# Row maxima as a 97th row of the contraction in a fused decoder layer pair

## What is computed

```python
x = _layernorm(x + _L0_attn_ref(x, ...), axis=-1)       # splat attention, 256 keys, head width 16
x = _layernorm(x + _L0_xattn_ref(x, ctx_512, ...), axis=-1)   # cross attention, 120 keys, width 16
x = _layernorm(x + _L0_ffn_ref(x, ...), axis=-1)
x = _layernorm(x + _L1_attn_ref(x, ...), axis=-1)       # causal attention, 256 keys, width 16
x = _layernorm(x + _L1_xattn_ref(x, ctx_512, ...), axis=-1)   # self (256 keys) and cross (120), width 32
x = _layernorm(x + _L1_ffn_ref(x, ...), axis=-1)
```

```python
attn = jnp.einsum('bqhd,bkhd->bhqk', Q, K) * SCALE
attn = jax.nn.softmax(attn, axis=-1)
O = jnp.einsum('bhqk,bkhd->bqhd', attn, V)
```

## Time and profile before

| what | value |
|---|---|
| median of 3 runs | 3753.8 us (3750.38 to 3755.05) |
| the profiled execution's own time | 3753.18 us |
| its span, first to last instruction | 3751.0 us |
| mean granted clock of TensorE, share of 2.4 GHz | 0.924 |
| instructions | 89546 |

### The profile page before, as it was taken

One profiled execution on the slowest core, in us unless ns is written; L12 is line 12 of the kernel. 1 busy time (PEld: TensorE's weight loads), 2 busy tenths in 40 slices (PEclk: granted clock), 3 DMA queues, 4 the chain that ended last, 5 costly groups with the idle time before them and its releaser, 6 DMA issues. The chain is left out here.

```text
span 3751.0 us, 89546 instructions
## 1 busy us (share of the span) xinstructions
PE 3123.4 (83%) x34864; PEld 2456.7 (65%) x34864; DVE 2699.4 (72%) x6135; ACT 2105.0 (56%) x4254; POOL 978.4 (26%) x1793
## 2 busy tenths in 40 slices
PE   1989888888888978888988888798988897988886
PEld 1767666766676757766766666676756676766664
DVE  6868676777676767767777667687777677768765
ACT  4745665555556554564565555646655556466542
POOL 1312341122223321231133222212343113124310
PEclk9999899999899989989998988999999999999987
DMA  6211211112112121121121111212121112122110
GB/s 199 70 55 56 79 61 53 45 45 67 55 54 72 48 62 41 50 67 55 48 72 56 54 53 38 70 45 71 60 67 60 39 41 68 48 62 71 60 37 6
DMA packets 362006, 221.49 MB, mean 59 GB/s; under 512 B 102497, under 2 KB 333298, under 8 KB 361586
## 3 DMA queue, kind: packets, MB, share of 16 engines
q1 hardware_dynamic: 361586, 215.76, 19.0%
HBM read 122.23 MB, written 93.32 MB: 57 GB/s over the span
## 5 line engine op out<-in xcount | busy, mean ns | idle before, releaser
L1158 ACT ACTIVATE p<-bank,p_log 128x512 f32<-128x512 f32 (+2 forms) x1280 | 748.3, 585 | 1122.3 <-PE bank L850 1019.3
L1712 POOL TENSOR_TENSOR prob<-p,prob 120x256 f16<-120x256 f32 (+2 forms) x512 | 451.7, 882 | 1650.9 <-ACT prob L1159 1650.5
L1159 ACT ACTIVATE prob<-bank,p_log 128x512 f16<-128x512 f32 (+2 forms) x1280 | 749.3, 585 | 0.0
L1417 DVE TENSOR_REDUCE negm<-bank 128x2 f16<-128x512 f32 (+1 forms) x1280 | 674.8, 568 | 98.9 <-PE bank L813 89.2
L1347 DVE TENSOR_TENSOR prob<-p,prob 128x512 f16<-128x512 f32 (+2 forms) x768 | 485.6, 641 | 92.6 <-ACT prob L1159 88.5
L720 PE MATMUL bank<-w_exp,ident_h 128*128 128x512 f16 x1280 | 418.9, 411 | 101.7 <-DMA k_ring<-k_heads 85.8
L829 PE MATMUL bank<-q_ring,k_ring 80*128 80x256 f16 (+4 forms) x2048 | 445.1, 284 | 40.8 <-ACT raw L1105 14.4
L850 PE MATMUL bank<-ident_h,negm 128*128 128x256 f16 (+2 forms) x2560 | 440.7, 259 | 0.0
L1721 POOL TENSOR_SCALAR_AFFINE_SELECT probm<-prob 128x128 f16<-128x128 f16 x1024 | 326.7, 357 | 308.9 <-DVE prob L1347 308.9
L813 PE MATMUL bank<-k_ring,q_ring 80*128 80x256 f16 (+4 forms) x2560 | 368.5, 259 | 34.8 <-DVE negm L1417 34.2
L813 PEld LDWEIGHTS bank<-k_ring,q_ring 80*128 80x128 f16 (+1 forms) x2560 | 236.5, 104 | 234.2 <-issue 51.5
(11 more groups left out here) (299 smaller groups left out, 6190.1 us busy)
## 6 DMA issues: line engine op xcount, KB each, us to landing
q_ring<-q_heads SPq DMA_DIRECT2D x768, 40.0 KB, 2.2
q_heads<-q_made SPq DMA_DIRECT2D x96, 256.0 KB, 2.4
k_heads<-k_made SPq DMA_DIRECT2D x96, 256.0 KB, 2.3
q_ring<-q_heads SPq DMA_DIRECT2D x512, 48.0 KB, 2.2
k_ring<-k_heads SPq DMA_DIRECT2D x512, 40.0 KB, 2.2
q_heads<-q_made SPq DMA_DIRECT2D x144, 128.0 KB, 1.8
k_heads<-k_made SPq DMA_DIRECT2D x144, 128.0 KB, 1.8
k_ring<-k_heads SPq DMA_DIRECT2D x256, 48.0 KB, 2.2
```

What stands on the lines that cost most here:

```text
L1158: act(p32[0:n, g % PBUF32, 0:cols], ps[0:n, 0:cols], ACT.Exp, bias=p_log[0:n, :], scale=a.scale)
L1159: act(prob[0:n, 0, g % PBUF, 0:cols], ps[0:n, 0:cols], ACT.Exp, bias=p_log[0:n, :], scale=a.scale).then_inc(a_done, one(a_done))
L1417: v.tensor_reduce(negm[:, h * NT:(h + 1) * NT], ring_v[bank_of(e, v_full)][:, :].rearrange("p (t n) -> p t n", t=NT)[:, :, 0:ATTNS[k].keys ...
L1712: g.tensor_tensor(prob[0:n, 1, m % PBUF, 0:cols], p32[0:n, m % PBUF32, 0:cols], prob[0:n, 0, m % PBUF, 0:cols], ALU.subtract).then_inc(pp_ ...
```

## The change

The maximum becomes a row of the contraction. `q_ring` and `k_ring` get a 97th row: ones in `k_ring`, set once, and the negated maxima in `q_ring`. So the exact scores need no product of their own for the maxima. To bring the maxima from columns (a query per partition) to a row (a query per column), TensorE makes four products per pair with the identity, each of 128 columns, into a bank of `ring_a` (`maxima_to_row`), and ScalarE copies one partition of that bank, 512 elements, to row 96 of `q_ring` (`row_of_maxima`). Both are the last piece of the step in which the maxima are taken. The wait for the maxima moves from `exact_scores` to `maxima_to_row`, and `exact_scores` waits for ScalarE's copy.

For this the 16-wide heads are stacked to 96 rows as well, with a third plane of zeros, so the fills carry 96 rows and twelve stores of zeros at the start stand in the place of eight. For causal heads the mask product now closes the group. The core of the diff:

```diff
-        self.stacked = 96 if dim == 32 else 80
+STACKED = 96
...
-        q_ring, k_ring = (sb(f"{what}_ring", [96, SLOTS, PAIR, TOK], F16) for what in "qk")
+        q_ring, k_ring = (sb(f"{what}_ring", [STACKED + 1, SLOTS, PAIR, TOK], F16) for what in "qk")
...
-                        for plane in (3, 4):
+                        for plane in (3, 4, 5):
...
+                step(g.memset(k_ring[STACKED:STACKED + 1, :, :, :], 1.0))
...
+                def maxima_to_row(pair):
+
+                    ps = slot("a", "row", pair[0] // PAIR)
+                    e.wait_ge(*moved("max", pair[1]))
+                    for at, g in enumerate(pair):
+                        for i in range(NT):
+                            column = ORDER[g][2] * NT + i
+                            c = (at * NT + i) * P
+                            last = mm(ps[:, c:c + P], negm[:, column:column + 1].broadcast_to([P, P]), ident_h[:, :],
+                                      start=(at, i) == (0, 0), stop=(at, i) == (PAIR - 1, NT - 1))
+                    last.then_inc(a_full, one(a_full))
...
                         ps = slot("a", "p", g)
+                        if g == pair[0]:
+                            e.wait_ge(*moved("row", g // PAIR))
                         for j, (k0, n) in enumerate(a.key_tiles):
                             i0 = j * P if a.causal else 0
-                            mm(ps[0:n, j * TOK:j * TOK + TOK - i0], kk[:, k0:k0 + n], q[:, i0:TOK],
-                               start=j == 0, stop=False)
-                        e.wait_ge(*moved("max", g))
...
-                            last = mm(o, negm[:, h * NT + i:h * NT + i + 1].broadcast_to([P, n]), moving,
-                                      start=False, stop=i == NT - 1)
+                            last = mm(ps[0:n, j * TOK:j * TOK + TOK - i0], kk[:, k0:k0 + n], q[:, i0:TOK],
+                                      start=j == 0, stop=not a.causal and k0 + n == a.keys)
...
+                    if n < len(ORDER):
+                        maxima_to_row((n, n + 1))
...
+                def row_of_maxima(m):
+
+                    e.wait_ge(a_full, upcoming(e, a_full))
+                    ps = ring_a[bank_of(e, a_full)]
+                    act(q_ring[STACKED:STACKED + 1, m % SLOTS, :, :].rearrange("o h n -> o (h n)"),
+                        ps[STACKED:STACKED + 1, :], ACT.Copy).then_inc(a_done, one(a_done))
...
+                    if n < len(ORDER):
+                        row_of_maxima(n // PAIR)
```

More of the change, by code:

```diff
@@ L320, in decoder @@
         made = {what: pair(f"{what}_made", 4, TOK) for what in "qk"}
-        q_ring, k_ring = (sb(f"{what}_ring", [96, SLOTS, PAIR, TOK], F16) for what in "qk")
-        heads16 = {what: nc.dram_tensor(f"{what}_heads16", (2, 5, P, 2 * TOK), F16).ap() for what in "qk"}
-        heads32 = {what: nc.dram_tensor(f"{what}_heads32", (2, 3, P, 4 * TOK), F16).ap() for what in "qk"}
+        q_ring, k_ring = (sb(f"{what}_ring", [STACKED + 1, SLOTS, PAIR, TOK], F16) for what in "qk")
+        heads16 = {what: nc.dram_tensor(f"{what}_heads16", (2, STACKED // 16, P, 2 * TOK), F16).ap() for what in "qk"}
+        heads32 = {what: nc.dram_tensor(f"{what}_heads32", (2, STACKED // 32, P, 4 * TOK), F16).ap() for what in "qk"}
         val = [pair(f"v{s}", NT * HEADS, 33) for s in range(SETS)]
@@ L509, in _ @@
                 e.wait_ge(w_ready[1], w_count[1])
-                e.wait_ge(zeros_stored, 16 * 8)
+                e.wait_ge(zeros_stored, 16 * 12)
             @block.gpsimd
@@ L793, in values, with operands @@
                             token_major(ws, col, 512, src, n_in, [tile], "a", *what, by="dve")
-                def operands(g):
+                def operands(g, rows):
                     a, h = ATTNS[ORDER[g][0]], ORDER[g][2]
                     slot_of, at = g // PAIR % SLOTS, h % PAIR
-                    return q_ring[0:a.stacked, slot_of, at, :], k_ring[0:a.stacked, slot_of, at, 0:a.keys]
+                    return q_ring[0:rows, slot_of, at, :], k_ring[0:rows, slot_of, at, 0:a.keys]
                 def row_scores(pair):
@@ L839, in exact_scores @@
-                        for i in range(NT):
-                            if a.causal:
-                                o = ps[0:n, 0:P] if i == 0 else ps[0:n, P:TOK + P].rearrange("p (j c) -> p j c", j=NT)
-                                times = 1 + i
-                            else:
-                                o, times = rows[:, 0:len(a.key_tiles), i * P:i * P + P], len(a.key_tiles)
-                            moving = ident_h[:, :]
-                            if a.causal and i == 0:
-                                pass
-                            else:
-                                moving = moving.rearrange("p (a n) -> p a n", a=1).broadcast_to([P, times, P])
-                            last = mm(o, negm[:, h * NT + i:h * NT + i + 1].broadcast_to([P, n]), moving,
-                                      start=False, stop=i == NT - 1)
+                            last = mm(ps[0:n, j * TOK:j * TOK + TOK - i0], kk[:, k0:k0 + n], q[:, i0:TOK],
+                                      start=j == 0, stop=not a.causal and k0 + n == a.keys)
@@ L852, in exact_scores @@
+                        if a.causal:
+                            blocks = ps[:, :].rearrange("p (j c) -> p j c", j=NT)[:, :, 0:P]
+                            last = mm(blocks, ident_h[:, :], mask_k[:, :].rearrange("p (a n) -> p a n", a=1
+                                                                                    ).broadcast_to([P, NT, P]),
+                                      start=False, stop=True)
                         last.then_inc(a_full, one(a_full))
```

14 lines of the change are left out of this document (4 added, 10 removed).

## The result

The changed kernel takes a median of **3995.6 us** (3992.4 to 3996.5, four runs) beside 3752.6 us for the kernel before: ratio **1.065, 95% interval 1.063 to 1.066**, so 243 us slower. The profiled execution took 3995.17 us, its span 3993.0 us, the mean granted clock was 0.905.

What follows compares the result with a forecast made beforehand. TensorE, 83% busy, was taken as nearest to a bound, with hand-overs between engines deciding. Terms -68 + 170 + 74 + 2 = +178 us on 3753 gave 3930 us, range 3790 to 4120 (8 times in 10).

Steps and rivals of the forecast that it cites:

- term 1: TensorE's products: 1280 products of 256 columns become 128 wide, each 0.053 us shorter, -68 us if TensorE is always on the path.
- term 4: Row products wait for VectorE's second maximum at their step's end: put at 0 us, up to 0.3 us a light step uncovered.
- term 2: Exact scores, exponentials, turns and copy form a chain of ScalarE's busy time + 1.0 us per step: +170 us.
- term 3: Late between work on ScalarE delays the copy: 92 stalls of 0.8 us, +74 us, bounds 0 and 296.
- rival of refunded stalls: Stalls give VectorE and ScalarE rest that TensorE later need not wait out: 3687 us, chance 0.09.
- term 5: A third slot per pair in the ring of three banks, each bank needed one user sooner: put at 0 us.
- term 6: Small things: 96-row fills, twelve stores of zeros instead of eight, memset of ones, 97-row contraction: +2 us in all.
- The clock: Rival: spread idle time lowers TensorE's mean clock from 0.924 to 0.848, up to 4210 us, chance 0.10; sign: under 0.88.
- sign of a shorter busy time: Sign that the forecast is right: TensorE's busy time over the kernel at about 3055 us, from 3123.
- Closer coupling: Rival: banks and VectorE tie steps closer, every pair paying 0.8 us: 4225 us at most, some 4080 at half, chance 0.14.
- Nothing visible: Rival: the copy always lies under fillers and row scores with ScalarE ready: within 0.2% of 3754 us, chance 0.03.
- light steps against the context: Sign that the forecast is right: light steps whose keys are the context take near 2.75 us (1.75 + 1.0).

## Why the prediction was right, and where it wasn't

The forecast was 3930 us within 3790 to 4120; it came to 3996. The sign, the loop as the largest part and its length in a light step were right. That the sum came so near is in good part luck. Against the table above, term 1 is off by 77 us, a term of 73 is missing and term 4 is off by 57, all too low; terms 2 and 3 together are 139 too high.

**TensorE's products (term 1, -68 us): failed.** The step multiplied a spacing by a count "if TensorE were on the path all the time". But 214 us taken away brought nothing, with the clock that followed. The page's 83% for TensorE had been read as the nearest thing to a bound. By the Trainium skill ("TensorE: Matmul & The Clock Gate", back-to-back issue gap) the gain would have been 37 us, and that was too much as well. The spacing was not the question: two rows of the changed kernel's timeline, four products of 128 columns from 1582.59 to 1582.81, give 0.055 us each, as predicted.

**The row as mere work: a term that was missing.** The sum had no entry for copy, bank and row products apart from the loop; they cost 73 us. The right entry in the place of -68 was about +82.

**The loop through ScalarE (term 2, +170) and the tail (term 3, +74): right mechanism, mis-sized.** "ScalarE's busy time + 1.0 us" gave 3.4 us for the light step; it is 3.59. The copy was to overlap the exponential ahead of it by 0.11 us, but starts 0.03 us behind its end (1583.31 and 1583.34), and TensorE wakes 0.14 us after the copy, not 0.10. The page has the copy at 589 ns (0.58 forecast), and ScalarE's busy time at 2479.6 us (2425 forecast, at 0.5 us a copy; 640 x 0.589 = 377 is nearer). But what the wait costs as a whole is 105 to 122 us, not 244; no run separates the tail (term 3) from the rest. The steps of the sample can be compared one by one. The first stretch of the earlier trace rows, the same eight steps now:

```profile
1577.33:1580.48 3.15, 2.40 (x30) 1.79 (x30) 2.40 (x6) 2.65 (x6) 0.67 (x1) 1.00 0.25 72
1580.48:1584.07 3.59, 2.15 (x27) 1.51 (x27) 3.32 (x8) 3.01 (x5) 0.68 (x1) 1.00 0.24 66
1584.07:1593.27 9.20, 8.20 (x86) 6.39 (x87) 4.41 (x8) 5.55 (x11) 1.63 (x2) 1.00 0.22 68
1593.27:1598.32 5.05, 4.05 (x55) 3.37 (x55) 4.23 (x11) 4.58 (x10) 2.83 (x3) 1.00 0.03 8
1598.32:1606.69 8.37, 6.39 (x75) 5.32 (x76) 4.79 (x10) 8.26 (x17) 2.37 (x2) 1.00 0.31 94
1606.69:1615.74 9.05, 8.47 (x90) 6.41 (x91) 4.18 (x8) 7.13 (x12) 1.15 (x1) 1.00 0.08 24
...
1620.91:1629.18 8.27, 4.84 (x61) 3.62 (x61) 6.45 (x26) 3.81 (x7) 1.85 (x2) 0.84 0.27 79
```

Against the earlier trace rows the steps changed by +0.29, +1.11, -0.30, +0.95, +0.72, -0.48, 0 and -1.23 us. What terms 1 and 2 forecast is the loop's share less the 0.21 us of shorter products: +0.19, +0.92, -0.21, +0.36, +0.69, -0.07, -0.21 and -0.21, together +1.46 against +1.06 measured. The second stretch, now from 1033.63 to 1080.91, grew by 1.79 us where 1.10 was forecast. So in the 16 steps the forecast was near (2.56 against 2.85 us), but 2.85 us in 16 steps is 114 us in 640, and the whole trace has 234: the sample held less than half of the loss. The near match in it is one of totals, not of causes: the measured growth holds the row's work and the wait at the maxima as well, which were put at nothing.

Two of the long steps got clearly *shorter*: 9.53 is 9.05, 9.50 is 8.27. That is the rival of refunded stalls, real but partial. That an engine which rests in a light step has less arrears in the heavy one is a reason that fits. Over the whole trace, pairing each step of before with its own after: the 147 steps that took under 3 us before got 142 us longer together, the 355 between 3 and 8 us got 130 longer, the 137 that took over 8 us got 38 shorter. (Between the kernel before and the one with 96 rows, which take the same time, the three groups differ by +5, -9 and -5 us.)

**The wait for VectorE's maxima (term 4, 0 us): failed, it cost 39 to 57.** The reason given was that light steps get 0.9 us longer anyway and VectorE fits in. In the light step that held, though the wait itself is there (1.22 us). It doesn't hold in other steps, the longest such wait being 5.5 us. The bound that the text kept, 0.3 us in light steps alone, was put in the wrong place.

**The third slot in the ring (term 5, 0 us): 14 us**, good to 9, measured in the kernel without the two waits and as a difference of two rings' prices; far below the bound of 296.

**Rows and setup (term 6, +2 us): somewhat low.** Ninety-six rows alone changed nothing in the total. The first exact scores stand 8 us later in the changed kernel and 6 us later with 96 rows alone (96.4 us). Some 3 us of that is scatter from one execution to the next: with one filler and with three, whose start is otherwise as before, they stand at 93.8 and 93.2 us, not 90.2.

**The rivals.** The clock fell to 0.905, above the 0.88 that would have pointed to it. TensorE was busy for 3177 us, not 3055, so the text's own sign of a shorter busy time failed, by the clock for the most part: counted at full clock (the busy time at 1.2 GHz taken half) it is 2854 us, where it was 2883, so 29 us less and not 68. A low mean clock doesn't bring the loss by itself: without the row it was 0.892, TensorE idled less in its steps than in the changed kernel (652 against 708 us), and the time was 3762 us. The Trainium skill's rule ("TensorE: Matmul & The Clock Gate", on HAM oscillation) is that idle gaps cost clock. The changed kernel agrees with it, 186 us more idle time at a clock lower by 0.019; that the loss comes by it no run here shows. Closer coupling (4080 to 4225) didn't come true as a time; its two pieces were there at a fraction of their bounds, 39 to 57 us at VectorE and 14 at the bank. "Nothing visible" fell with 373 of 640 pairs waiting. Of the other signs, the copy's 0.58 us and the light steps of 3.3 to 3.6 came out; the wait of TensorE's products for the copy is the largest entry, at 229.2 us where some 250 were named; light steps against the context, put near 2.75, are 3.23 and 2.66 us in the sample.

## What to carry to other kernels

Before a gain is put down for work taken from the busiest engine, ask whether that engine's queue has idle time at this very place, and if possible remove the work alone or add filler of the same size: here 83% busy was worth nothing downwards and 21 of 138 us upwards. A value that goes from TensorE through another engine's in-order queue and back in the same step ties the two queues into a loop whose length is that engine's whole busy time in the step plus about 1 us here; that price is found in the short and middling steps, and a part of it is refunded in the long ones, so a few sampled steps are a poor base for the sum. Moving such a copy ahead of other work whose results are waited for can shorten the step that it stands in and lose more in those behind it, as it did here by 67 us.

## What the runs showed of the hardware

- On ScalarE a copy from one partition saves next to nothing over many: 1x512 from a bank took 589 ns, beside 580 for 16x512 and 606 for 128x512 (L1093 into `inT`, before), while 128x256 took 401 (L1093 into `v`, before). On VectorE 1x512 from a bank took 697 ns.
- Two such copies in a row on ScalarE start 0.50 us apart (1666.28 and 1666.78), though one that follows an exponential without a wait starts only after its end, by 25 ns in the median of 180.
- TensorE's granted clock follows its work closely (0.892, 0.902, 0.924, 0.935 for -214, -138, 0 and +138 us of products) while the time of the kernel stands still within 22 us: less work, at a lower clock, fills nearly the same time.
- A contraction over 97 rows costs what one over 80 or 96 does: the exact scores' products have a median duration of 273 ns before and 272 after, and four with 256 columns and 97 rows take 0.43 us from the first start to the next work (1580.48 to 1580.91), 0.11 each as before.
